# Edge-attribute sums moved from the two sum passes into the two relation passes, and shorter layer ends, in a four-layer graph network

## The reference, cut to what matters

```
h = relu(layernorm(x)); x = x + L0(h)   # attention over the edges
h = relu(layernorm(x)); x = x + L1(h)   # relations: per type, mean of h[src] @ W_r over dst, and of h[dst] @ W_r over src
h = relu(layernorm(x)); x = x + L2(h)   # GINE
h = relu(layernorm(x)); x = x + L3(h)   # edge convolution
# L2, with a self loop of attribute (4, 0, ..., 0) added to every node:
agg  = h + segment_sum(h[far] + edge_attr_16 @ W_edge + b_edge)
out  = relu(batchnorm(agg @ W1 + b1)) @ W2 + b2
# L3:
out  = relu(segment_sum(h[src] @ W + b + edge_attr_6 @ We + be, dst))
```

## Time and profile before

| what | us |
|---|---|
| median of 3 runs (lowest, highest) | 15916.97 (15910.03, 15919.94) |
| the profiled execution's own time | 15913.28 |
| its span in the trace | 15911.1 |
| PE busy / DVE busy / ACT busy / POOL busy | 10293.0 / 9384.4 / 2592.3 / 11144.0 |

### The profile page before, as it was taken

How to read it: one execution, slowest core, us unless ns; L and a number is a source line. 1 busy time by engine, 2 the same in 40 slices (tenths; PEclk the granted TensorE clock), 3 DMA queues, 4 the chain that set the end, 5 groups by cost and what they waited for, 6 DMA issues and landing times. The chain is left out here.

```text
span 15911.1 us, 207629 instructions
## 1 busy us (share of the span) xinstructions
PE 10293.0 (65%) x60197; PEld 8268.7 (52%) x60197; DVE 9384.4 (59%) x30337; ACT 2592.3 (16%) x6666; POOL 11144.0 (70%) x11474
## 2 busy tenths in 40 slices
PE   6766647777777775555554555553777768777777
PEld 2222226666666663344444444443666665666666
DVE  9977758888788777755555555554333332333331
ACT  0011114444444442211111111111000002000000
POOL 4777777777777776677777777774777760677773
PEclk9966669999999997755555555555555555555555
DMA  2011122222222224322223222223222232222223
GB/s 80 11 46 52 48 62 69 69 68 69 69 70 69 69 69 110 112 58 57 57 57 54 62 61 62 61 61 55 61 62 62 62 54 65 64 58 58 58 57 39
DMA packets 675304, 988.05 MB, mean 62 GB/s; under 512 B 232206, under 2 KB 473564, under 8 KB 674076
## 3 DMA queue, kind: packets, MB, share of 16 engines
q0 software_dynamic: 392896, 680.65, 18.5%
q1 hardware_dynamic: 281308, 294.11, 6.1%
HBM read 795.08 MB, written 178.86 MB: 61 GB/s over the span
## 5 line engine op out<-in xcount | busy, mean ns | idle before, releaser
L1528 DVE TENSOR_TENSOR acc<-banks,acc 128x145 f32 (+1 forms) x3328 | 1011.3, 304 | 2712.3 <-PE banks L1512 2345.9
L722 POOL DMA_INDIRECT far_sum_dst<-table_h,recs_sum_dst x1664 | 1578.1, 948 | 1026.0 <-DMA recs_sum_dst<-rec_dst 519.2
L621 POOL DMA_INDIRECT rec_dst<-stage_dst_sort,row_dst_sort x1563 | 1569.9, 1004 | 694.5 <-issue 475.6
L722 POOL DMA_INDIRECT far_sum_src<-table_h,recs_sum_src x1664 | 1576.5, 947 | 652.2 <-issue 426.3
L722 POOL DMA_INDIRECT far_att<-table_qv,recs_att x1664 | 1626.5, 977 | 532.5 <-issue 506.5
L722 POOL DMA_INDIRECT far_rel_dst<-table_xw,recs_rel_dst x1664 | 1590.0, 956 | 562.8 <-issue 506.9
L1404 DVE TENSOR_TENSOR acc<-banks,acc 128x128 f32 x3328 | 969.8, 291 | 1694.6 <-PE banks L1359 1331.7
L722 POOL DMA_INDIRECT far_rel_src<-table_xw,recs_rel_src x1664 | 1588.5, 955 | 537.4 <-issue 506.8
L1511 PE MATMUL banks<-far_sum_src,hot_sum_src 128*128 128x128 f32 x3328 | 1285.8, 490 | 745.7 <-issue 579.5
L1511 PE MATMUL banks<-far_sum_dst,hot_sum_dst 128*128 128x128 f32 x3328 | 1286.2, 490 | 640.4 <-issue 579.6
L1359 PE MATMUL banks<-far_rel_dst,hot_s_rel_dst 128*128 128x128 f32 x3328 | 851.4, 438 | 1045.1 <-DVE share_rel_dst L1394 708.2
(11 more groups left out here) (304 smaller groups left out, 23233.4 us busy)
## 6 DMA issues: line engine op xcount, KB each, us to landing
table_xw<-xw_rel_tables SPq DMA_DIRECT2D x98, 512.0 KB, 2.7
far_att<-table_qv,recs_att POOLq DMA_INDIRECT x1664
far_rel_dst<-table_xw,recs_rel_dst POOLq DMA_INDIRECT x1664
far_rel_src<-table_xw,recs_rel_src POOLq DMA_INDIRECT x1664
far_sum_src<-table_h,recs_sum_src POOLq DMA_INDIRECT x1664
far_sum_dst<-table_h,recs_sum_dst POOLq DMA_INDIRECT x1664
rec_dst<-stage_dst_sort,row_dst_sort POOLq DMA_INDIRECT x1563
rec_src<-moved_att,row_src POOLq DMA_INDIRECT x1248
```

Source lines behind the costliest of these rows:

```text
L621: e.indirect_dma_start(out=flat_dst, out_offset=bass.IndirectOffsetOnAxis(ap=row["dst"][:, c + i:c + i + 1], axis=0), in_=stage["dst"][:, ...
L722: e.indirect_dma_start(out=self.far[:, g % RING, t, :], out_offset=None, in_=table, in_offset=bass.IndirectOffsetOnAxis(ap=index, axis=0)) ...
L1528: e.tensor_tensor(acc[:, bass.ds(at[t], 1), :], bank(g0, t).unsqueeze(1), acc[:, bass.ds(at[t], 1), :], ALU.add).then_inc(k.s_sum, 1)
```

## The change: what it does

1. **Attributes in the relation passes.** ACT and DVE split each block's attributes (float32) into three bfloat16 parts: ACT copies the high part, DVE subtracts (`rested`), ACT copies the middle part, DVE subtracts (`low`); that is 2 ACT and 2 DVE instructions per block, one to three blocks ahead. PE multiplies the bfloat16 mask of each tile by (1, high, middle, low): 4 more products per group, of 19 columns (dst) or 49 (src). DVE adds each to a new tensor `more`, right behind the tile's add to `acc`. The banks are dealt anew: three for the sums instead of four, and three for the look-ups, beside which the new products lie.
2. **Sum passes.** The second product of each tile is gone, and `acc` has 128 columns. Beside the pass, once in 16 groups, PE turns 4 windows of `more`, ACT copies them, and PE multiplies them by the weights (written three times). For src DVE adds the result to `acc` and b2 to `x`; for dst ACT copies it out and SP stores it to `conv_rows`. Five small parameter loads stand ahead of the records' loads in SP's order.
3. **`gine_tables`.** The 14 adds are no longer all done first, the copy and the clears are gone (ACT writes `acc` itself), and chunk c+1 is measured before chunk c is settled.
4. **`gine_end`.** The attribute turn, its copy and its product are gone from the first walk, b2's product from the second; turning runs one step ahead over four banks; the clear of `acc` moves to POOL, behind the last turn. In the second walk ACT scales two steps ahead (`warmed(j + 2)`, between `deviation(j)` and the ReLU of j); SP's order is as before.
5. **`edge_conv_end`.** Only turn, one copy, one product, and two DVE instructions (add the fetched `conv_rows`, then max and add `x`), over four banks; the turn one step ahead.

```diff
 # relation_pass, tensor
+                    for t in range(GT):
+                        e.matmul(added[g2 % 3][:, t, :], hot[:, g2 % 4, t, :], fine[:, c % 3, first + t, :], start=True, stop=True)
                     e.wait_ge(k.s_flat, q0 + g2 + 1)
 # relation_pass, vector
+            def rested(c):
+                e.wait_ge(k.s_high, b0 + c + 1)
+                e.wait_ge(k.s_low, b0 + c)
+                e.tensor_tensor(rest[:, :, :], attrs(c), parts(c, 0), ALU.subtract).then_inc(k.s_rest, 1)
+            def low(c):
+                e.wait_ge(k.s_mid, b0 + c + 1)
+                e.tensor_tensor(parts(c, 2), rest[:, :, :], parts(c, 1), ALU.subtract).then_inc(k.s_low, 1)
...
                     for t in range(GT):
+                        mine = more[:, bass.ds(at[t], 1), :]
                         e.wait_ge(k.s_sum, GT * (p0 + g0) + t)
-                        e.tensor_tensor(acc[:, bass.ds(at[t], 1), :], sums[g0 % 4][:, t:t + 1, :], acc[:, bass.ds(at[t], 1), :],
+                        e.tensor_tensor(acc[:, bass.ds(at[t], 1), :], sums[g0 % 3][:, t:t + 1, :], acc[:, bass.ds(at[t], 1), :],
                                         ALU.add).then_inc(k.s_sum, 1)
+                        e.wait_ge(k.s_more, GT * (q0 + g0) + t)
+                        e.tensor_tensor(mine, added[g0 % 3][:, t:t + 1, :], mine, ALU.add).then_inc(k.s_more, 1)
+                if g3 is not None and g3 % RG == 0 and g3 // RG + 1 < BLOCKS:
+                    rested(g3 // RG + 1)
+                if g3 is not None and g3 % RG == 2 and g3 // RG + 1 < BLOCKS:
+                    low(g3 // RG + 1)
 # sum_pass, tensor
-                    e.matmul(bank(g, t)[:, 0:F], hot[:, b, t, :], st.far[:, b, t, :], start=True, stop=True)
-                    i = e.matmul(bank(g, t)[:, F:n_all], hot[:, b, t, :], st.rows(g, ONE, ONE + extra)[:, t, :], start=True, stop=True)
+                    i = e.matmul(sums[g % 4][:, t, :], hot[:, b, t, :], st.far[:, b, t, :], start=True, stop=True)
 # sum_pass, vector
+                        if spent:
+                            e.wait_ge(k.s_spent, spent)
...
+                    j = beside(g0, 12) if gine else None
+                    if j is not None:
...
+                        e.tensor_tensor(acc[:, w0:w0 + n, :], acc[:, w0:w0 + n, :], k.psum[6 + j % 2][:, 0:n * P].rearrange("p (n f) -> p n f", f=F),
+                                        ALU.add).then_inc(k.s_spent, 1)
...
+                        e.tensor_tensor(k.x[:, w0:w0 + n, :], k.x[:, w0:w0 + n, :], over(bias[:, :], n), ALU.add).then_inc(k.s_bias, 1)
 # gine_tables, vector
             for c in range(chunks):
+                if c + 1 < chunks:
+                    begin(c + 1)
+                settle(k, e, moments[:, c % 3, :, :], C7, norms + c)
 # gine_end, tensor
-                for i in range(n):
-                    e.matmul(k.psum[2 + b][:, i * P:(i + 1) * P], k.acc17[:, w0 + i, 0:F], k.ident[:, :], start=True, stop=False)
-                    t = e.matmul(k.psum[2 + b][:, i * P:(i + 1) * P], wc[:, :], et[:, b, i * P:(i + 1) * P], start=False, stop=True)
-                t.then_inc(s_agg, 1)
-                e.wait_ge(s_aggt, j + 1)
+                if j + 1 < fours_n:
+                    turn(j + 1)
...
+                e.wait_ge(k.s_aggt, j + 1)
 # gine_end, scalar
             warmed(0)
+            warmed(1)
             for j, (w0, n) in enumerate(WIN4):
                 b = j % 2
-                if j + 1 < len(WIN4):
-                    warmed(j + 1)
+                deviation(k, e, moments[:, b, 0:n, 1], norms + j)
+                if j + 2 < fours_n:
+                    warmed(j + 2)
                 if j >= 2:
                     e.wait_ge(s_out[b], 16 * (j // 2))
-                relu_rows(k, e, k.x[:, w0:w0 + n, :], h[:, b, :, :], moments[:, b, :, :], n, norms + j)
+                e.wait_ge(k.s_norm, norms + j + 1)
+                for i in range(n):
+                    e.activation(h[:, b, i, :], k.x[:, w0 + i, :], ACT.Relu, bias=moments[:, b, i, 0:1],
+                                 scale=moments[:, b, i, 1:2]).then_inc(k.s_h, 1)
+        def gpsimd(e):
+            e.wait_ge(k.s_agg, fours_n)
+            e.memset(k.acc_flat[:, 0:(W + 1) * F], 0.0)
 # edge_conv_end, tensor
+                for i in range(n):
+                    t = e.matmul(k.psum[4 + j % 4][:, i * P:(i + 1) * P], aggt[:, j % 2, i * P:(i + 1) * P], w3[:, :], start=True, stop=True)
```

More of the change, by code:

```diff
@@ L56 @@
 CS = ATT + 16
+ATTRS = {"dst": 6, "src": 16}
+MORE = {s: 1 + 3 * n for s, n in ATTRS.items()}
 NONE = -1.0e30
@@ L1378, in vector @@
         def vector(e):
+            def rested(c):
[5 more added lines that the diff above has]
+                e.tensor_tensor(parts(c, 2), rest[:, :, :], parts(c, 1), ALU.subtract).then_inc(k.s_low, 1)
+            e.memset(fine[:, :, :, 0:1], 1.0).then_inc(k.s_one, 1)
+            e.memset(more[:, :, :], 0.0).then_inc(k.s_one, 1)
+            e.wait_ge(k.s_one, o0 + 2)
+            if side == "src":
+                e.memset(more[:, 0:W, 0:1], 1.0).then_inc(k.s_one, 1)
+                e.memset(more[:, 0:W, 1:2], 4.0).then_inc(k.s_one, 1)
+                e.wait_ge(k.s_one, o0 + 4)
+            rested(0)
+            low(0)
             for g3, g1, g0 in steps((3, 1, 0)):
@@ L1463, in sync @@
                 e.wait_ge(k.s_h, h0 + (c + 1) * C7)
-                e.dma_start(rows[:, c * C7:(c + 1) * C7, :], h[:, c % 2, :, :]).then_inc(s_out[c % 2], 16)
-            for b in range(2):
-                e.wait_ge(s_out[b], 16 * len(range(b, chunks, 2)))
+                e.dma_start(rows[:, windows(c), :], k.acc[:, windows(c), :]).then_inc(s_out, 16)
+            e.wait_ge(s_out, 16 * chunks)
         with k.nc.Block() as block:
@@ L1473, in gine_tables, with sum_pass @@
         k.rows += W
-def sum_pass(k, side, acc, extra):
-    n_all = F + extra
+def sum_pass(k, side):
+    a = k.a
     with ExitStack() as ctx:
@@ L1482, in sum_pass, with beside @@
         hot = sb("hot", [P, RING, GT, P])
-        win, p0 = k.win[side], k.passes * GROUPS
-        def bank(g, t):
-            at = t % 2 * n_all
-            return k.psum[g % 4 * 2 + t // 2][:, at:at + n_all]
-        def sync(e):
+        win, acc, p0 = k.win[side], k.acc, k.passes * GROUPS
+        sums = [k.psum[i].rearrange("p (t f) -> p t f", t=GT) for i in range(4)]
+        more, n_more, n_att = k.more[side], MORE[side], ATTRS[side]
+        gine = side == "src"
+        wc, bias = sb("wc", [n_more, F]), sb("bias", [P if gine else 1, F])
+        et = sb("et", [n_more, 2, G4 * P])
+        kept = None if gine else sb("kept", [P, 2, G4 * P])
+        f0, bias0 = (0, 0) if gine else (len(WIN4), len(WIN4))
+        pars = 16 * 5 * (1 if gine else 2)
+        def beside(g, step):
+            j, i = divmod(g, BESIDE)
+            return j if i == step and j < len(WIN4) else None
+        def sync(e):
+            edge, weights = ("L2_gnn_b_edge", "L2_gnn_W_edge") if gine else ("L3_gnn_b", "L3_gnn_We")
+            e.dma_start(wc[0:1, :], row_of(a[edge])).then_inc(k.s_par, 16)
+            for i in range(3):
+                e.dma_start(wc[1 + i * n_att:1 + (i + 1) * n_att, :], a[weights]).then_inc(k.s_par, 16)
+            e.dma_start(bias[:, :], row_of(a["L2_gnn_b2"]).to_broadcast([P, F]) if gine else row_of(a["L3_gnn_be"])).then_inc(k.s_par, 16)
             for c in range(BLOCKS):
@@ L1493, in sync @@
                 st.load(e, c)
+                if not gine and c >= 7 and (c - 7) % 4 == 0:
+                    j = (c - 7) // 4
+                    w0, n = WIN4[j]
+                    e.wait_ge(k.s_spent, f0 + j + 1)
+                    e.dma_start(k.conv[:, w0:w0 + n, :], kept[:, j % 2, 0:n * P]).then_inc(k.s_parked[j % 2], 16)
+            if not gine:
+                for b in range(2):
+                    e.wait_ge(k.s_parked[b], 16 * len(range(b, len(WIN4), 2)))
         def gpsimd(e):
```

343 lines of the change are left out of this document (209 added, 134 removed).

## The result

The changed kernel takes 15523.23 us (median of 4 runs, 15518.23 to 15534.48) and the kernel before, on the same chip, 15913.5 us (4 runs, 15908.97 to 15919.94): a ratio of 0.9754, 95% interval 0.9743 to 0.9765. The profiled execution took 15519.78 us, its span is 15518.0 us. The forecast was 15570.

| stretch | before | after | difference | forecast |
|---|---|---|---|---|
| start to first relation gather | 6619.9 | 6611.6 | -8 | 0 |
| two relation passes | 4221.8 | 4205.5 | -16 | +10 |
| to first src sum gather | 146.3 | 92.4 | -54 | -54 |
| src sum pass | 2082.3 | 2131.2 | **+49** | +8 |
| to first dst sum gather (`gine_end`) | 520.1 | 286.9 | **-233** | -188 |

What follows compares the result with a forecast made beforehand. POOL's gathers were taken to pace the passes, with every microsecond counting outside them; terms -56 - 181 - 7 - 138 + 4 - 3 + 10 + 19 + 8 = -344 took the profiled 15913 to 15569, forecast 15570, range 15520 to 15630 (8 in 10: 15500 to 15750).

Steps and rivals of the forecast that it cites:

- The passes' pace: All four passes: POOL's gathers set the pace, one every 1.26 us in relation passes and 1.25 us in sum passes.
- Relation passes, DVE side: Relation passes: DVE's step becomes 3.7 us, under the 5.04 us of four gathers, hidden behind POOL; cost 0.
- the lower bound: Relation passes: each new add to `more` fits into the gap, only the last shows, +0.1 us per group.
- Collisions in the relation passes: Relation passes: the mask write moves later and lengthens some gathers by 0.1 to 0.3 us, 5 us per pass.
- `gine_tables`: Stage `gine_tables`: 115.4 us becomes 59 as chunks are no longer serial between DVE and ACT, gain 56.
- First walk: `gine_end`, first walk: PE stays the bound at 4.3 us per step, 105 us in all, gain 181.
- a rival at 15510: The ends give more: clock rises to 1.0, collisions stay away; chance 0.14 together with ends giving less (15610).
- Second walk: `gine_end`, second walk: by SP's order each step is a store, fetch, scaling, ReLU round trip of 7.65 us; gain 7.
- `edge_conv_end`: Final stage: 208.2 us becomes 70 at 2.6 us per step, gain 138; 128 if DMA sets 3.0.
- Sum passes: Sum passes: masks hit a tenth of dst groups, +19; src delayed by `s_spent`, safer, adds to `x` may hit, +8.
- the 60 that the prediction allowed: Sign for the passes: under 60 of 1664 gathers over 1 us.
- The lock on every group: Mask lengthens a gather in each group: one pass 15780 us, chance 0.12; two passes or more 15967, chance 0.05.

Runs made afterwards that it cites:

- four-instruction delay: Four statistics instructions on DVE ahead of each mask in both sum passes, against the changed kernel: 19893.26 us (one run), unedited 19849.83 us on that chip.

## Why the prediction was right

The time came within 0.3% of the forecast, and luck had a part in it: the first walk came out 46 us under its term, the relation passes 26, `edge_conv_end` and the start 9 and 8, and the src sum pass 41 over it. The passes' pace and the second walk's round trip were right as mechanisms; the clock and the src masks were not.

- **Relation passes, DVE side**: right, and the lower bound was the right choice. The new adds lie in the gap; a step of DVE is 1420.71 / 416 = 3.4 us busy of 5.04.
- **Collisions in the relation passes**: +10 forecast, -16 measured. Held gathers fell in the dst pass (61 to 34) and rose in the src pass (53 to 60), where each was held for less (18.4 us in all to 12.3); the mask moved, but not onto the gathers.
- **`gine_tables`**: -56 and +2 for the loads, measured -54.
- **First walk**: the term that was mis-sized. I kept 3.57 us for W1 and 0.87 for the turns, the low clock's durations; at 1.00 they are 1.8 and 0.45 us, 2.4 us a step instead of 4.3. The walk is 59 us instead of 105. I had the rise of the clock as part of a rival at 15510. The runs show that two waits in each step bring the clock down, and further with 17-row products. The old walk had both. The wait for ACT's copy and the 17-row products left with the attribute sums, and that gave the clock back, though not shown is how much of it each did: with the other wait put back in (the turns right ahead of their copy) it stays at 1.00. Turning one step ahead gave 20 us more, the covered idle time.
- **Second walk**: -7 forecast, 194.0 to 186.5 measured; the step of 7.65 us was 7.5 to 7.9. The working by SP's order held, and one moved fetch proves it.
- **`edge_conv_end`**: -138, measured -148 with its tail. I sized PE at 2.55 us a step, by the low clock again; it needed 1.33 at 1.00. DVE waits for `out` 19 times, 18.2 us in all, so the row buffer's round trip sets the step, at 2.3 us, which the forecast had named beside PE's 2.55.
- **Sum passes**: dst right (+19, measured +18), src wrong (+8, measured +49). I let the wait for `s_spent` make the src pass safer; instead 176 gathers were held there, 85 in dst, both over the 60 that the prediction allowed. The adds to `x`, which the +8 was for, held 15 and cost 4 us; the masks cost the rest. The mechanism, a mask that moves toward a gather's start, was right; that `s_spent` protects was wrong. No run tells why the masks held twice as many gathers in src as in dst (161 and 85).
- **Rivals**: none came true as a whole; the clock's half of the last one did. The lock on every group did not form: the mask's place wanders, from 0 to 1.2 us behind a gather's start. The four-instruction delay, run on a slower chip, did not form it either.

## What to carry to other kernels

Where GpSimd's gathers pace a stage, give DVE's wide instructions beside them at most one SBUF input (a constant row in PSUM is enough), keep clears of SBUF away from them, and do this rather than tune their moment. Where PE bounds a walk at the low clock, and a change takes out waits and small products, size the rest at both levels before summing: here the same products took half as long. Where a queue's order holds a fetch behind a store that waits for a result, the step is their round trip; one more fetch ahead was worth 80 to 82 us here.

## What the hardware showed unexpectedly

The kernel before took 15914 and 15922 us on two chips and 20320 to 20365 us on three others, while a gather took 0.94 us and an add 0.29 on both. In a stretch of the latter PE has no record for 10 us, and DVE and then POOL wait for something that the profile calls "remote"; by the kernel's order it is PE's products (timeline of the run with SP's order changed):

```profile
14830.00 2.08 PE L1630 MATMUL banks<-far_sum_src,hot_sum_src 128*128 128x128 f32 x8 [10.89 <-DVE hot_sum_src L1663]
14839.80 1.59 DVE L1672 TENSOR_TENSOR acc<-banks,acc 128x128 f32 x4 [9.86 <-remote]
14839.93 0.94 POOL L748 DMA_INDIRECT far_sum_src<-table_h,recs_sum_src  x1 [4.17 <-remote]
```

In the kernel before on such a chip PE does have records in such stretches, single ones with idle time between that is put down to "issue", so that it does not stop but gets slow:

```profile
14982.08 0.37 PE L1511 MATMUL banks<-far_sum_src,hot_sum_src 128*128 128x128 f32 x1 [1.03 <-issue]
14982.79 0.37 PE L1511 MATMUL banks<-far_sum_src,hot_sum_src 128*128 128x128 f32 x1 [0.34 <-issue]
```

What holds PE up there stays open. A cut in the gathers' time was worth nothing on such a chip (passes of 2382 and 2379 us with 2 held gathers, of 2381 and 2378 with 338); a cut in the number of PE's products seems to be worth something. The gain in us differs between the chips (390 and 470); the ratios, 0.9754 and 0.9771, can't be told apart by their intervals.
